# A two-stage kernel on one core: GpSimd's step in the second stage is put in another order

## The chip, the cores and the metric

The kernel runs on one core of a Trainium2 chip. The metric is device time in microseconds (us), the median of the runs shown; everything that the kernel does in one launch counts.

## The reference

`x` is 16 images of 512 channels, 64 x 64 pixels, float32. Two layers follow each other, each with a group normalisation (32 groups of 16 channels) in front and a residual add behind:

```python
x = x + _L0_conv_ref(_gn(x), W, bias)     # 5x5 self-correlation descriptor, 1x1 convolution, relu
x = x + _L1_conv_ref(_gn(x), w1, b1, w2, b2)

def _L1_conv_ref(x, w1, b1, w2, b2):      # KERNELS = 1, 3, 5, 7, 9, 11, 13
    gap = jnp.mean(x, axis=(2, 3))
    hmid = jax.nn.relu(jnp.einsum('bc,ec->be', gap, w1) + b1)
    s = jax.nn.relu(jnp.einsum('be,ce->bc', hmid, w2) + b2)
    q_s = jnp.clip(jnp.floor(s), 0, n_k - 2).astype(jnp.int32)
    q_b = q_s + 1
    ...
    return frac_b * b_out + frac_s * s_out + x   # two max pools of each plane, mixed
```

In the second layer each of the 8192 planes (one channel of one image) gets a score. The score picks two neighbouring pool sizes of the seven, and the result is a weighted sum of the two max-pooled planes and the plane itself.

## The kernel before

**Stage one** (0 to about 2610 us of the span) does the first layer, image by image, and writes each plane twice to device memory: the plane itself (`y_planes`) and the plane after a row-wise maximum (`wide_planes`). **A short middle part** (to about 2690 us) scores the planes, gives each one of six classes (0 to 5, by its smaller pool size), sorts them by class and packs them in tiles of 128 planes of one class. There are 72 tile numbers (`NT`), of which 67 hold planes; the last 5 are empty.

**Stage two** is the one that the change touches. It goes through the tiles, in the order of the classes. Five engines work side by side, each with an instruction order written out by hand, tied by semaphores. Tile `t` uses plane buffer `t % 4` (`bufs`, 4 buffers), and there is one `source` buffer only. What each does:

- GpSimd (`POOL`) issues the transfers, all of them indirect DMAs of its own queue. `gather(t, b)`: clears the record slot (L506), copies the tile's plane numbers (L507), waits for that copy, reads the tile's class, then issues the gather of the records (L511) and of the planes (L514, 128 rows of 16 KB). `gather_source(t, b)`: waits until ScalarE has taken the source of the tile before (`s_ypad`), copies indices (L528), issues the gather of row maxima into `source` (L531). For classes 2 to 5 this is 128 rows of 16 KB, for classes 0 and 1 all rows but one are out of bounds. `scatter(t, b)`: waits for the eight results of the tile (`s_res`), then issues the write to `out` (L539), again 128 rows of 16 KB. In front of `gather(t + 2)` the engine waits until the scatter of tile `t - 2`, which had the same buffer, has landed (`written`).
- ScalarE (`ACT`), in its step `t`: `pad_plane(t + 1)` copies tile `t + 1` into the padded buffer `ypad` (L673 to L675), out of its own plane buffer for classes 0 and 1 and out of `source` for the others. Then `results(t - 1)` moves the eight finished banks of tile `t - 1` from PSUM to its buffer (L695), and `diagonals(t + 1)` makes the weights (L687, L688).
- VectorE (`DVE`) computes the two pools of a tile from `ypad` as a chain of elementwise maxima (all at L1062), 6 to 12 of them by class. It starts when `ypad` is ready. Half-way it has no more need of `ypad` and says so (`s_rows`).
- TensorE (`PE`) mixes: per bank two matmuls (class 0) or three (L1403, L1405, L1407), each one instruction of the program and two records of the trace. Bank `b` of a tile waits until ScalarE has emptied it of the tile before.

`pad_plane` starts with the three waits on which much rests:

```python
act.wait_ge(gathered[u], turns_done(t, u))   # record and plane gathers of tile t landed
if not (isinstance(t, int) and t == 0):
    act.wait_ge(s_rows, t)                   # VectorE has done with ypad of tile t - 1
act.wait_ge(sourced, (t + 1) * 16)           # source gather of tile t landed
```

GpSimd's order of a step is given by the function `step`:

Of the kernel before, what the change touches and what calls it, by code (L numbers as in the profile page):

```python
# [41 lines left out]
BUFS = 4  # L42
# [46 lines left out]
def build(nc, x, wt, wturn, bias, w1t, b1, w2t, b2, consts, out):  # L89
# [5 lines left out]
    NT = -(-(NC + NCLS - 1) // BUFS) * BUFS  # L95
# [15 lines left out]
    with ctx:  # L111
# [328 lines left out]
        def _(pool):  # L440
# [60 lines left out]
            def class_of(t):  # L501
                return pool.value_load(cls_i[0:1, bass.ds(t, 1)], min_val=0, max_val=NCLS)  # L502

            def gather(t, b):
                pool.sem_inc(s_issue, 1)
                pool.memset(recs_in[:, b, :], 0.0)  # L506
                pool.tensor_copy(idx[:, b:b + 1], ids_i[:, bass.ds(t, 1)]).then_inc(s_idx, 1)  # L507
                pool.wait_ge(s_idx, t + 1)
                pool.sem_inc(s_issue, 1)
                with pool.If(class_of(t) < NCLS):  # L510
                    pool.indirect_dma_start(out=recs_in[:, b, :], out_offset=None, in_=rec_dram[:, :],  # L511
                                            in_offset=bass.IndirectOffsetOnAxis(ap=idx[:, b:b + 1], axis=0),
                                            bounds_check=NPL - 1, oob_is_err=False).then_inc(gathered[b], 16)
                    pool.indirect_dma_start(out=bufs[:, b, :], out_offset=None, in_=y_dram[:, :],  # L514
                                            in_offset=bass.IndirectOffsetOnAxis(ap=idx[:, b:b + 1], axis=0),
                                            bounds_check=NPL - 1, oob_is_err=False).then_inc(gathered[b], 16)
                with pool.Else():
                    pool.dma_start(bufs[0:1, b, 0:REC], rec_dram[0:1, :]).then_inc(gathered[b], 16)
                    pool.dma_start(recs_in[0:1, b, :], rec_dram[0:1, :]).then_inc(gathered[b], 16)

            def gather_source(t, b):

                if not (isinstance(t, int) and t == 0):
                    pool.wait_ge(s_ypad, t)
                    pool.sem_inc(s_issue, 1)
                    pool.wait_ge(sourced, t * 16)
                pool.sem_inc(s_issue, 1)
                pool.tensor_copy(src_idx[:, b:b + 1], src_ids[:, bass.ds(t, 1)]).then_inc(s_src, 1)  # L528
                pool.wait_ge(s_src, t + 1)
                pool.sem_inc(s_issue, 1)  # L530
                pool.indirect_dma_start(out=source, out_offset=None, in_=wide_dram[:, :],  # L531
                                        in_offset=bass.IndirectOffsetOnAxis(ap=src_idx[:, b:b + 1], axis=0),
                                        bounds_check=NPL - 1, oob_is_err=False).then_inc(sourced, 16)

            def scatter(t, b):
                pool.wait_ge(s_res, (t + 1) * 8)
                pool.sem_inc(s_issue, 1)  # L537
                with pool.If(class_of(t) < NCLS):  # L538
                    pool.indirect_dma_start(out=out_rows[:, :],  # L539
                                            out_offset=bass.IndirectOffsetOnAxis(ap=idx[:, b:b + 1], axis=0),  # L540
                                            in_=bufs[:, b, :], in_offset=None,
                                            bounds_check=NPL - 1, oob_is_err=False).then_inc(written[b], 16)
                with pool.Else():
                    pool.dma_start(no_out[bass.ds(t, 1), :], bufs[0:1, b, 0:REC]).then_inc(written[b], 16)  # L544

            def step(t, u):

                if not (isinstance(t, int) and t + 1 >= NT):
                    gather_source(t + 1, (u + 1) % BUFS)
                if not (isinstance(t, int) and t < 2):  # L550
                    pool.wait_ge(written[(u + 2) % BUFS], ((t - 2) // BUFS + 1) * 16 if isinstance(t, int)
                                 else turn_of(t, u - 2))
                if not (isinstance(t, int) and t + 2 >= NT):
                    gather(t + 2, (u + 2) % BUFS)
                if not (isinstance(t, int) and t < 1):
                    scatter(t - 1, (u - 1) % BUFS)

            gather(0, 0)
            gather_source(0, 0)
            gather(1, 1)  # L560
            for u in range(BUFS):
                step(u, u)
            with pool.Fori(1, NT // BUFS - 1) as g:
                def turn_of(t, back):

                    return (g + (1 if back >= 0 else 0)) * 16
                for u in range(BUFS):
                    step(g * BUFS + u, u)
            for u in range(BUFS):
                step(NT - BUFS + u, u)  # L570
# [867 lines left out]
```

## Time and profile before

| | |
|---|---|
| median of 3 runs | 4451.67 us (4446.97 to 4456.05) |
| the profiled execution | 4448.36 us |
| its span | 4446.7 us |
| busy in the span: TensorE, VectorE, ScalarE, GpSimd | 88%, 80%, 43%, 51% |
| stage two with its tail, from the first L673 (2687.3 us) to the end of the span | 1759 us |

The span is the profiled part of one execution; the execution's own time is 1.7 us longer. Engines of the trace are PE (TensorE), PEld (its weight loads), DVE (VectorE), ACT (ScalarE), POOL (GpSimd) and SP. L531 is line 531 of the kernel. A row of a timeline has the start, the duration, the engine, line and operation; in brackets stands the engine's idle time before it and what ended it.

### The profile page before, as it was taken

The numbers are of one execution on the slowest core, as the hardware profiler recorded it, in microseconds if no ns is written. First come the engines' busy times: TensorE is split into PE (matmuls) and PEld (weight loads), VectorE is DVE, ScalarE is ACT, GpSimd is POOL, SyncE is SP. The second block draws the span as 40 slices with busy tenths as digits, with TensorE's granted clock in tenths as the row PEclk, the third lists the DMA queues.
The fourth block names the chain that finished last, engine by engine and source line by source line (L and its number), as shares of the span: only waits on it lengthen the run. The fifth ranks groups of instructions, "written<-read, shape, count | busy, mean of one in ns | idle before, by whom it ended". The sixth has DMA issues, their size and how long they took to land. (4 is left out here: it accounts for less than half of the span.)

```text
span 4446.7 us, 76741 instructions
## 1 busy us (share of the span) xinstructions
PE 3932.6 (88%) x23656; PEld 2159.5 (49%) x23657; DVE 3557.4 (80%) x3528; ACT 1897.6 (43%) x2964; POOL 2279.6 (51%) x1793
## 2 busy tenths in 40 slices
PE   5999999999999999999999965789888888888785
PEld 3556555555555555655566642334333333333332
DVE  5878888788887878888888766699866799999993
ACT  3444444444454544444444403443433333433332
POOL 3555555555555655555565514355544444556442
PEclk9999999999999999999999977899998999989897
DMA  4444344544544444444453334545555566565551
GB/s 183 151 173 176 137 168 167 176 150 156 195 149 159 173 150 167 177 150 155 176 173 132 121 79 172 202 174 190 198 219 234 197 234 246 227 243 211 224 212 50
DMA packets 252235, 781.08 MB, mean 176 GB/s; under 512 B 98150, under 2 KB 98150, under 8 KB 229990
## 3 DMA queue, kind: packets, MB, share of 16 engines
q1 hardware_dynamic: 219600, 417.85, 26.9%
q0 software_dynamic: 32288, 358.95, 20.9%
q8 instruction: 176, 2.88, 0.3%
q14 instruction: 171, 1.40, 0.1%
HBM read 428.22 MB, written 409.08 MB: 188 GB/s over the span
## 5 line engine op out<-in xcount | busy, mean ns | idle before, releaser
L1062 DVE TENSOR_TENSOR arena<-arena 128x2048 f32<-128x2048 f32 (+5 forms) x539 | 1442.4, 2695 | 262.2 <-ACT arena L675 223.0
L1403 PE MATMUL psum<-arena 128*128 128x512 f32 x1072 | 608.3, 651 | 293.4 <-ACT arena L695 213.0
L1208 PE MATMUL psum<-arena 128*128 128x256 f16 (+1 forms) x6344 | 754.6, 273 | 57.4 <-DVE arena L808 44.2
L447 POOL TENSOR_TENSOR arena<-arena 128x512 f16<-128x512 f32 x512 | 720.8, 1415 | 147.1 <-ACT arena L597 141.0
L1231 PE MATMUL psum<-arena 128*128 128x512 f16 x2048 | 776.5, 379 | 0.0
L1233 PE MATMUL psum<-arena 128*128 128x512 f16 x2048 | 776.2, 379 | 0.0
L1232 PE MATMUL psum<-arena 128*128 128x512 f16 x2048 | 776.2, 379 | 0.0
L673 ACT ACTIVATE arena<-arena 128x4096 f32 x67 | 242.4, 3619 | 1051.7 <-issue 1051.7
L1208 PEld LDWEIGHTS psum<-arena 128*128 128x128 f16 x6344 | 600.3, 101 | 177.6 <-DVE arena L808 71.7
L456 POOL TENSOR_TENSOR arena<-arena 128x512 f32 (+1 forms) x512 | 635.0, 1272 | 9.0 <-ACT arena L611 6.2
L820 DVE BATCH_NORM_STATS2 bny<-arena 128x6 f32 (+1 forms) x512 | 355.6, 694 | 340.0 <-POOL arena L456 326.7
L611 ACT ACTIVATE arena<-psum,bias_sb 128x512 f32<-128x512 f32 x512 | 338.1, 686 | 581.3 <-POOL arena L456 380.1
L1407 PE MATMUL psum<-arena 128*128 128x512 f32 x1072 | 578.9, 623 | 0.0
L466 POOL CAST arena<-arena 128x128 f16<-128x128 f32 x128 | 37.3, 291 | 999.3 <-DVE arena L852 999.3
L1403 PEld LDWEIGHTS psum<-arena 128*128 128x128 f32 x1072 | 216.1, 208 | 589.7 <-issue 316.7
L1405 PE MATMUL psum<-arena 128*128 128x512 f32 x896 | 494.2, 635 | 0.0
L595 ACT ACTIVATE arena<-arena,gbias,grstd 128x512 f32 (+1 forms) x512 | 413.3, 807 | 48.6 <-POOL arena L447 45.9
L597 ACT ACTIVATE arena<-arena,gbias,grstd 128x512 f16 (+1 forms) x512 | 411.3, 803 | 0.0
L539 POOL DMA_INDIRECT out<-arena x67 | 115.4, 1722 | 544.2 <-issue 544.2
L1407 PEld LDWEIGHTS psum<-arena 128*128 128x128 f32 x1072 | 218.0, 203 | 287.7 <-issue 287.7
L808 DVE TENSOR_TENSOR arena<-psum,cst 128x256 f32<-128x256 f32 x496 | 287.1, 579 | 74.8 <-PE psum L1208 60.3
L695 ACT ACTIVATE arena<-psum,arena 128x512 f32<-128x512 f32 x536 | 319.0, 696 | 57.5 <-PE psum L1407 46.0
(161 smaller groups left out, 4324.0 us busy)
## 6 DMA issues: line engine op xcount, KB each, us to landing
arena<-in_x SPq DMA_DIRECT2D x64, 2048.0 KB, 13.2
wide_planes<-arena SPq DMA_DIRECT2D x128, 1024.0 KB, 5.4
y_planes<-arena SPq DMA_DIRECT2D x64, 2048.0 KB, 7.6
arena<-arena SPq DMA_DIRECT2D x1536, 8.0 KB, 1.8
arena<-wide_planes,arena POOLq DMA_INDIRECT x72
arena<-plane_records,arena POOLq DMA_INDIRECT x67
arena<-y_planes,arena POOLq DMA_INDIRECT x67
out<-arena POOLq DMA_INDIRECT x67, 7.9
```

The lines of the kernel that those rows point to most:

```text
L447: pool.tensor_tensor(gl[:, ct, slot], g32[:, ct % 2, :], gh[:, ct, slot], ALU.subtract).then_inc(s_gl, 1)
L456: pool.tensor_tensor(y, y, relu[:, o % 2, :], ALU.add).then_inc(s_added, 1)
L595: act.activation(g32[:, ct % 2, :], piece, ACT.Identity, bias=gbias[:, ct:ct + 1], scale=grstd[:, ct:ct + 1])
L597: act.activation(gh[:, ct, (c % RING) * CW:(c % RING + 1) * CW], piece, ACT.Identity, bias=gbias[:, ct:ct + 1], scale=grstd[:, ct:ct + 1]) ...
L1062: ins = dve.tensor_tensor(dst, a, b, ALU.max)
L1208: return pe.matmul(dst, w, m, start=(k == 0), stop=(k == nk - 1))
L1231: pe.matmul(dst, h, gh[:, ct, slot], start=(ct == 0), stop=False)
L1232: pe.matmul(dst, h, gl[:, ct, slot], start=False, stop=False)
L1233: last = pe.matmul(dst, l, gh[:, ct, slot], start=False, stop=(ct == CT - 1))
L1403: pe.matmul(dst, diag[:, s, 0, :], bufs[:, u, b * CW:(b + 1) * CW], start=True, stop=False)
L1405: pe.matmul(dst, diag[:, s, 1, :], small[:, s, b * ROWS:(b + 1) * ROWS, 1:W + 1], start=False, stop=False)
L1407: pe.matmul(dst, diag[:, s, 2, :], big[:, s, b * CW:(b + 1) * CW], start=False, stop=True)\
```

## The change

Only GpSimd's program changes, in `step` and in the lines in front of the loop. A step had: source gather of the tile one ahead; wait for the scatter of tile `t - 2`; record and plane gathers of the tile two ahead; scatter of tile `t - 1`. It now has: source gather of the tile two ahead; scatter of tile `t - 1`; wait for the scatter of tile `t - 2`; record and plane gathers of the tile two ahead. The source gather of tile 1 is issued in front of the loop. The number of transfers and their sizes stay as they were, and no wait is added to or taken from the helpers.

```diff
             def step(t, u):
 
-                if not (isinstance(t, int) and t + 1 >= NT):
-                    gather_source(t + 1, (u + 1) % BUFS)
+                if not (isinstance(t, int) and t + 2 >= NT):
+                    gather_source(t + 2, (u + 2) % BUFS)
+                if not (isinstance(t, int) and t < 1):
+                    scatter(t - 1, (u - 1) % BUFS)
                 if not (isinstance(t, int) and t < 2):
                     pool.wait_ge(written[(u + 2) % BUFS], ((t - 2) // BUFS + 1) * 16 if isinstance(t, int)
                                  else turn_of(t, u - 2))
                 if not (isinstance(t, int) and t + 2 >= NT):
                     gather(t + 2, (u + 2) % BUFS)
-                if not (isinstance(t, int) and t < 1):
-                    scatter(t - 1, (u - 1) % BUFS)
 
             gather(0, 0)
             gather_source(0, 0)
             gather(1, 1)
+            gather_source(1, 1)
```

## Rows read from the trace of the kernel before

**Rows 1.** Busy time by stretch (window, length, engines, PEclk, DMA, GB/s): classes 0 to 5.

```profile
2735.20:2925.70 190.50, 147.45 (x293) 61.91 (x291) 127.12 (x56) 89.41 (x136) 73.81 (x63) 0.87 0.51 199
2925.70:3189.10 263.40, 238.18 (x516) 103.16 (x517) 248.67 (x88) 109.77 (x165) 149.06 (x80) 0.93 0.50 185
3189.10:3523.40 334.30, 278.43 (x589) 119.16 (x587) 215.93 (x72) 119.19 (x180) 162.25 (x85) 0.91 0.55 213
3523.40:3806.80 283.40, 243.15 (x528) 104.35 (x528) 258.89 (x99) 109.30 (x166) 123.54 (x77) 0.95 0.62 237
3806.80:4094.70 287.90, 248.01 (x519) 106.26 (x520) 273.01 (x88) 109.22 (x166) 172.46 (x77) 0.91 0.58 225
4094.70:4337.80 243.10, 198.10 (x419) 84.81 (x418) 239.29 (x106) 90.08 (x136) 105.22 (x65) 0.91 0.57 218
```

**Rows 2.** Waits of 2735 to 4338 us; last row: who waited for L531, whole span.

```profile
ACT arena L673 <- issue: 972.0, 64, 18.9
...
POOL arena L506 <- DMA out<-arena: 140.2, 49, 6.8
...
  ACT arena L673: 1043.9, 66
```

**Rows 3.** Timeline of ScalarE over one tile of class 2.

```profile
3329.64 3.62 ACT L673 ACTIVATE arena<-arena 128x4096 f32 x1 [17.89 <-issue]
...
3333.47 0.40 ACT L675 ACTIVATE arena<-arena 128x256 f32 x1
3333.77 4.72 ACT L695 ACTIVATE arena<-psum,arena 128x512 f32<-128x512 f32 x8
...
3357.20 3.62 ACT L673 ACTIVATE arena<-arena 128x4096 f32 x1 [17.60 <-issue]
```

**Rows 4.** Timeline of GpSimd over the same tile.

```profile
3340.14 1.87 POOL L539 DMA_INDIRECT out<-arena  x1 [9.23 <-issue]
3342.02 1.34 POOL L528 COPY arena<-arena 128x1 int32 x1
3344.29 4.53 POOL L531 DMA_INDIRECT arena<-wide_planes,arena  x1 [0.93 <-POOL arena L528]
3348.82 0.12 POOL L506 MEMSET arena<- 128x4 f32 x1
3348.87 3.52 POOL L507 COPY arena<-arena 128x1 int32 x1
3353.99 1.04 POOL L511 DMA_INDIRECT arena<-plane_records,arena  x1 [1.59 <-issue]
3355.33 0.99 POOL L514 DMA_INDIRECT arena<-y_planes,arena  x1 [0.30 <-issue]
```

**Rows 5.** VectorE in that tile: timeline, then its forms (busy, mean ns), in 3334 to 3352.5 us.

```profile
3334.11 18.24 DVE L1062 TENSOR_TENSOR arena<-arena 128x2112 f32<-128x2112 f32 x6 [9.62 <-ACT arena L675]
...
L1062 DVE TENSOR_TENSOR arena<-arena 128x4096 f32<-128x4096 f32 x2 | 8.8, 4424 | 0.2
L1062 DVE TENSOR_TENSOR arena<-arena 128x2048 f32<-128x2048 f32 x3 | 6.8, 2290 | 0.1
L1062 DVE TENSOR_TENSOR arena<-arena 128x2112 f32<-128x2112 f32 x1 | 2.4, 2359 | 9.6 <-ACT arena L675 9.6
```

**Rows 6.** Further VectorE forms: one tile of class 3, then one of class 4.

```profile
L1062 DVE TENSOR_TENSOR arena<-arena 128x1024 f32<-128x1024 f32 x3 | 3.6, 1223 | 0.1
L1062 DVE TENSOR_TENSOR arena<-arena 128x2176 f32<-128x2176 f32 x1 | 2.4, 2426 | 0.0
...
L1062 DVE TENSOR_TENSOR arena<-arena 128x2240 f32<-128x2240 f32 x1 | 2.5, 2491 | 0.0
```

**Rows 7.** L514 (ns: min/median/max) in the stretch of class 2, then of class 3.

```profile
L514 POOL DMA_INDIRECT arena<-y_planes,arena x13: 993/993/993, 3189.1 to 3521.5; - x13
...
L514 POOL DMA_INDIRECT arena<-y_planes,arena x11: 4104/4109/4112, 3548.6 to 3806.2; - x11
```

**Rows 8.** DMA rate, 3329 to 3358 us, in 40 slices of 0.725 us.

```profile
GB/s 0 2 1 271 113 316 407 497 407 407 429 45 0 0 0 0 0 0 362 362 362 362 362 678 407 0 0 0 271 136 452 429 452 429 384 339 2 1 249 113
```

## The prediction

> **What bounds the kernel now.** Stage one is untouched, so I first read the stretches of stage two [rows 1]. A tile is 15 ScalarE instructions (three of padding, eight of results, four of diagonals), so the stretches hold 9, 11, 12, 11, 11 and 9 tiles of classes 0 to 5, and a tile takes 21.2, 23.9, 27.9, 25.8, 26.2 and 27.0 us. VectorE is full in classes 1 and 5 (94 and 98%), but only 67% busy in class 0 and 65% in class 2, and no other engine is full there. So I read the waits [rows 2]: `pad_plane` (L673) waits 972 us in all, and in 66 of 67 cases what released it was L531, the source gather.
>
> The three timelines of one class 2 tile show the ring that follows. I count from the start of L673 at 3329.64. Padding ends at 4.2 and the results at 8.9 [rows 3]. The scatter starts at 10.5 and ends at 12.4, the index copy L528 at 13.7, the source gather's issue runs from 14.7 to 19.2 [rows 4], and the next L673 starts at 27.6, 8.4 after it (8.7 in the neighbouring tiles; I use 8.7 for the way from the end of an issue of 2 MB to the padding that waits for it). This ring is padding, results, scatter, source gather, padding. The plane gather of the tile behind it is issued at 25.7 to 26.7 and is not needed before the padding one period later: 27 us of slack.
>
> **How VectorE holds GpSimd.** With VectorE idle L514 takes 0.99 us in every case of class 2; in class 3, where a VectorE operation of 4.42 us runs over it, 4.11 [rows 7]. The single cases show the rule. VectorE's operations of the class 2 tile end at 6.8, 9.1, 11.5, 13.7, 18.25 and 22.7 (one of 2.36, three of 2.29, two of 4.42 from 4.47 on, with small gaps) [rows 5]. The copy L528 ends at 13.73 and the copy L507 at 22.75, each 0.05 after an operation's end; the scatter ends at 12.37 and L531 at 19.18, each 0.9 after one; the memset L506 isn't held (0.12) [rows 4]. So a copy lasts until the running operation ends, and an indirect issue until 0.9 after that. The shared port of the page "SBUF — State Buffer" of the Trainium skill is the name for this, but its section "Who interferes with whom" infers that a `tensor_tensor` does not hold descriptor generation. By it the indirect issues would take about 1 us always; the rows of L514 and L531 speak against it. It is rival B below.
>
> **The change, part by part.** Removed: GpSimd's wait for a landed scatter in front of L506, 140 us over 49 cases [rows 2]. It is beside the ring (the plane gather behind it has its slack), so it is worth nothing. In the new order the scatter of tile t - 2 is a whole period old when it is asked for, so this wait is gone.
>
> Moved forward: the source gather of tile t + 2 now waits only for the padding of t + 1. The end of padding comes at 4.2; L528 has some queue instructions in front of it, VectorE starts at 4.47, so I let the copy lose that race and be held to the end of the first operation. Bound: it wins, and the issue is over one operation sooner.
>
> Moved back: record and plane gathers of t + 2 now stand behind the scatter of t - 1, and that waits for results which ScalarE starts only after padding t + 1. Padding t + 2 waits for these gathers too. So there is a new ring: padding, results, scatter, L507, L511, L514, landing, padding. What was covered by 27 us of slack is now on it. In the rows its fixed parts are: 10.5 to the scatter's start, 1.6 from L507's end to L511, 0.3 from there to L514 [rows 4], 8.7 to the padding; between them each issue is held by the rule above. By class, ends counted from L673:
>
> Classes 0 and 1 (first operations 2.29 each, ends 6.8, 9.1, 11.3, 13.8, 16.1, 18.4): L528 to 6.8, L531 7.7 to 10.0, scatter 10.5 to 12.2, L507 to 13.9, L511 15.5 to 17.1, L514 17.4 to 19.3, next padding at 28.0. Nine tiles: 252.0 - 190.5 = +61.5. Eleven: 308.0 - 263.4 = +44.6.
>
> Class 2: L528 to 6.9, L531 to 10.0, scatter to 12.4, L507 to 13.7, L511 15.3 to 19.2, L514 19.5 to 23.6, padding at 32.3. Twelve tiles: 387.6 - 334.3 = +53.3.
>
> Class 3 starts with an operation of 4.42, then 2.43, three of 1.22, two of 2.29 [rows 5, 6]: ends 8.9, 11.4, 12.6, 13.9, 15.0, 17.3, 19.5. L528 to 8.9, L531 9.9 to 12.3, scatter to 13.5, L507 to 13.9, L511 15.5 to 18.3, L514 18.6 to 20.5: 29.2. Here the DMA queue decides. The slices show bursts of some 6.5 us for a gather (9 slices) and 5.1 for a scatter (7 slices) [rows 8]. Source, scatter and plane gather now follow each other in one queue within 9 us; if they run one behind the other, the padding comes at 12.3 + 8.7 + 5.1 + 6.2 = 32.3, and a burst that needs no start-up of its own saves about 1 us, so 30.3 to 32.3. I take 31.5. Eleven tiles: 346.5 - 283.4 = +63.1.
>
> Class 4 (4.42, 2.49, 2.42, three of 2.29 [rows 5, 6]: 8.9, 11.4, 13.9, 16.2, 18.5, 20.7): L531 to 12.4, scatter to 14.8, L507 to 16.3, L511 17.9 to 19.4, L514 19.7 to 21.6: 30.3; by the queue 30.4 to 32.4. I take 31.5 again: 346.5 - 287.9 = +58.6.
>
> Class 5: L531 to 10.0, plane issue to about 19.8: 28.5; by the queue 28.0 to 30.0; I take 29.2. VectorE needs 27 to 28 for such a tile, so it no longer bounds it, and the lead that padding had before the stretch's end, some 8.7 us, need not be worked off in the tail: 9 x 29.2 - 243.1 - 8.7 = +11.
>
> In front of class 0 the first two rings come from 13 and 22 us to about 22 and 30: +17, an estimate from the same parts. The five empty tiles at the end move nothing of size: 0.
>
> Sum: 61.5 + 44.6 + 53.3 + 63.1 + 58.6 + 11 + 17 = +309. The profiled execution takes 4448.4, so 4757; the median of the runs is 3.3 above it: 4760.
>
> The other price in this sum is the transfer. The page "DMA: Bandwidth & Descriptors" of the Trainium skill, section "Anatomy of one DMA — SWDGE (gpsimd) path", fits 2.0 us plus bytes over 436 GB/s; for 2 MB that would be 6.8 us, an estimate, in place of the 8.7 of the rows. With it each ring would be 1.9 us shorter and the sum about 120 us smaller, 4640.
>
> **Bounds.** Low: L528 wins its race in every tile, which ends L531 of classes 3 and 4 at 9.8, and bursts pack well: 28.3 in both, so 22 x 3.2 = 70 less: 4690. High: the scatter's queue instructions (1.66 us from the results to L539) start only when L531 has ended: each issue after it slips by one VectorE operation, 1.3 us in classes 0 to 2, some 2 to 3 in 3 and 4, 1.6 in 5: 32 x 1.3 + 22 x 2.5 + 9 x 1.6 = +111: 4870.
>
> **The rivals.**
> A, the forecast: the plane gather becomes the last thing that padding waits for, 4690 to 4870. Chance 0.88.
>
> B, VectorE does not hold the indirect issues, only the copies. Classes 0 and 1: L507 to 13.9, L514 to 17.8, padding at 26.5; class 2 about 28 by the queue, 3 and 4 about 30, 5 about 28. The sum is 48 + 28 + 0 + 47 + 42 + 0 + 17 = 182: 4634. Speaks against it: L514 and L531 at 4.1 and 4.5 us. Chance 0.05.
>
> C, the other side: the plane gather still lands before the source would have, and only the gain is left. For that its issue has to end by 21.2 - 8.7 = 12.5 in class 0 and by 19.2 in class 2. Then classes 0 to 5 would be bound by mixing and pools, about 17, 23, 23, 24, 25 and 27 us: a gain of 36 + 10 + 58 + 20 + 13 = 137, 4315. Against it: the scatter alone ends at 12.2, with two issues, a held copy and 1.6 us of queue still to come. Chance 0.03, with 0.01 more for no change (the change's two effects cancel).
>
> D, TensorE's clock. It was granted 0.91 of full in class 2 and a tile's 48 records cost 278.4 / 12 = 23.2 us busy [rows 1]. In a period of 32 it fits with room. If the longer idle times let the clock sit at its lower level throughout, a tile costs about 23.2 x 0.91 / 0.5 = 42 us, mixing bounds classes 1 to 5, and 54 tiles at some 46 give well over 5200. Nothing in the rows has it sit there while PE works most of the time. Chance 0.03.
>
> **How the numbers follow.** The likeliest case is A at 4760. The range is 4650 to 4870: the bounds of A, and toward B at the lower end. A change under 0.2% (about 9 us) is not to be told from none. Faster 0.03 (C), same 0.01, slower 0.96 (A, B, D).
>
> **What would show it.** In the changed profile L673 should be released by L514 or its landing and no more by L531; L531 should start some 8 after L673; L506 should wait for no landing; a tile of class 0 should take 28, of class 2 about 32, of 3 and 4 about 31. VectorE's idle time should rise by nearly the sum. I am wrong if the plane gather's issue ends before 17 in class 0, if the 8.7 us don't hold for a plane gather that runs right behind a scatter, or if the scatter starts later than 10.5 where L531 has ended before.

## The result and the profile after

The changed kernel takes 4817.25 us (median of 4 runs), the kernel before 4452.97 us beside it: a ratio of 1.082, 95% interval 1.080 to 1.084. That is 364 us slower; 4760 was forecast, with a range of 4650 to 4870. The profiled execution after has a span of 4811.8 us, 365.1 more than before.

First the stretches of stage two again, by class, as in [rows 1] (window, length, busy time of PE, PEld, DVE, ACT, POOL, then PEclk, DMA share, GB/s):

```profile
2752.10:3012.30 260.20, 146.11 (x288) 61.69 (x288) 131.25 (x56) 89.33 (x135) 103.24 (x63) 0.77 0.37 145
3012.30:3336.70 324.40, 250.78 (x528) 107.44 (x528) 242.61 (x86) 109.21 (x166) 134.28 (x77) 0.88 0.39 150
3336.70:3726.10 389.40, 275.77 (x576) 118.07 (x576) 215.91 (x72) 119.05 (x180) 182.16 (x84) 0.85 0.50 183
3726.10:4080.60 354.50, 252.79 (x528) 108.15 (x528) 261.55 (x99) 109.22 (x166) 138.27 (x77) 0.85 0.50 190
4080.60:4446.10 365.50, 254.03 (x528) 108.72 (x528) 274.94 (x88) 109.13 (x165) 165.81 (x77) 0.84 0.47 177
4446.10:4715.00 268.90, 208.60 (x432) 89.06 (x432) 245.11 (x108) 89.33 (x135) 101.02 (x63) 0.86 0.52 197
```

Every stretch is longer, and no engine's work accounts for it: VectorE is busy 1371.4 us over the six, against 1362.9 before [rows 1], and over the whole span VectorE is busy 3557 us as before, TensorE 28 us more (at a lower granted clock) and GpSimd 41 us more. The time is idle time. Its cause is in the waits of the two gathers (who waited for the line: us, times). L514 first, then L531, whole span:

```profile
  ACT arena L674: 1372.8, 65
...
  ACT arena L674: 71.8, 2
```

L674 is the first instruction of the padding (L673 before; lines behind the diff are one further down). Before, 66 paddings were released by the source gather [rows 2]. Now 65 are released by the plane gather L514 and two by the source gather. The ring of one class 2 tile, which answers to [rows 3] and [rows 4], ScalarE and then GpSimd:

```profile
3369.06 3.62 ACT L674 ACTIVATE arena<-arena 128x4096 f32 x1 [22.44 <-issue]
...
3373.19 4.71 ACT L696 ACTIVATE arena<-psum,arena 128x512 f32<-128x512 f32 x8
...
3401.61 3.62 ACT L674 ACTIVATE arena<-arena 128x4096 f32 x1 [22.59 <-issue]
```

```profile
3373.73 2.20 POOL L528 COPY arena<-arena 128x1 int32 x1 [13.49 <-ACT arena L676]
3376.82 2.29 POOL L531 DMA_INDIRECT arena<-wide_planes,arena  x1 [0.89 <-POOL arena L528]
3379.56 1.86 POOL L539 DMA_INDIRECT out<-arena  x1 [0.46 <-issue]
3381.42 0.12 POOL L506 MEMSET arena<- 128x4 f32 x1
3381.46 1.32 POOL L507 COPY arena<-arena 128x1 int32 x1
3384.52 3.73 POOL L511 DMA_INDIRECT arena<-plane_records,arena  x1 [1.73 <-issue]
3388.55 4.08 POOL L514 DMA_INDIRECT arena<-y_planes,arena  x1 [0.31 <-issue]
```

Counted from 3369.06: L528 ends at 6.9, L531 at 10.0, the scatter at 12.4, L507 at 13.7, L511 at 19.2, L514 at 23.6, the next padding starts at 32.55. GpSimd used to wait 140 us in front of L506 for a landed scatter [rows 2]; there is no such wait in this step. It now waits in front of L528 for the padding, 13.5 us in this tile: nothing is left for it to do meanwhile.

### The profile page after: what moved, and what is told of

It reads as the page before. It is cut to its first block and busy times, and to the rows that moved or that the text cites. A ratio compares the mean times of both kernels' runs of the same rounds, so it can differ in the third digit from the quotient of the medians.

```text
span 4811.8 us, 76741 instructions
## 1 busy us (share of the span) xinstructions
PE 3960.7 (82%) x23656; PEld 2169.7 (45%) x23657; DVE 3557.1 (74%) x3528; ACT 1894.0 (39%) x2964; POOL 2320.5 (48%) x1793
## 3 DMA queue, kind: packets, MB, share of 16 engines
q0 software_dynamic: 32288, 358.95, 19.7%
## 5 line engine op out<-in xcount | busy, mean ns | idle before, releaser
L1404 PE MATMUL psum<-arena 128*128 128x512 f32 x1072 | 624.9, 667 | 633.7 <-ACT arena L696 593.5
L674 ACT ACTIVATE arena<-arena 128x4096 f32 x67 | 242.3, 3616 | 1444.6 <-issue 1444.6
L528 POOL COPY arena<-arena 128x1 int32 (+1 forms) x72 | 191.3, 2657 | 957.0 <-ACT arena L676 942.7
L1408 PE MATMUL psum<-arena 128*128 128x512 f32 x1072 | 581.2, 625 | 0.0
L1406 PE MATMUL psum<-arena 128*128 128x512 f32 x896 | 503.5, 646 | 0.0
```

Of the source, the lines that this page charges most:

```text
L1404: pe.matmul(dst, diag[:, s, 0, :], bufs[:, u, b * CW:(b + 1) * CW], start=True, stop=False)
L1406: pe.matmul(dst, diag[:, s, 1, :], small[:, s, b * ROWS:(b + 1) * ROWS, 1:W + 1], start=False, stop=False)
L1408: pe.matmul(dst, diag[:, s, 2, :], big[:, s, b * CW:(b + 1) * CW], start=False, stop=True)\
```

## The experiments

All are edits of GpSimd's program in stage two, and one of VectorE's. The table gives, for each profile, us per tile of classes 0 to 5, worked out from the starts of the padding's first instruction (the 4th, 13th, 24th, 36th, 47th, 58th and 67th, difference over the number of tiles), and the whole. "-" in place of the interval: one execution. The kernel before, timed beside them, lay between 4438 and 4456 us, so a difference of less than some 15 us says nothing for a single execution. The groups are cut by count and are one tile off at the first two borders: the last tile of group 0 has the pools of class 1, and the last of group 1 those of class 2. Of the edits below, those with words in place of code are outlines.

| run | 0 | 1 | 2 | 3 | 4 | 5 | whole, us | ratio to before |
|---|---|---|---|---|---|---|---|---|
| kernel before | 21.2 | 23.9 | 27.9 | 25.8 | 26.2 | 27.0 | 4453 | 1 |
| changed kernel | 28.9 | 29.5 | 32.5 | 32.2 | 33.2 | 29.9 | 4817 | 1.080 to 1.084 |
| plane_moves_nothing | 22.4 | 23.7 | 26.0 | 27.7 | 27.7 | 27.1 | 4468 | - |
| scatter_moves_nothing | 27.9 | 28.1 | 32.4 | 29.2 | 30.6 | 28.8 | 4714 | - |
| short_pools | 28.4 | 28.6 | 30.0 | 32.1 | 32.4 | 29.8 | 4751 | - |
| prepare_ahead | 28.8 | 28.9 | 32.4 | 32.1 | 31.5 | 28.0 | 4768 | - |
| plane_late_only | 28.7 | 32.6 | 37.2 | 33.5 | 34.7 | 34.5 | 4975 | - |
| plane_before_scatter | 27.8 | 27.5 | 29.5 | 29.0 | 30.0 | 27.7 | 4655 | 1.044 to 1.048 |
| e1_scatter_moves_nothing | 25.8 | 25.7 | 28.3 | 27.0 | 28.0 | 27.5 | 4557 | - |
| plane_source_scatter | 19.7 | 24.3 | 25.8 | 27.5 | 28.6 | 27.6 | 4451 | 0.999 to 1.001 |
| issues_only_old_order | 21.3 | 24.1 | 25.5 | 25.8 | 25.5 | 27.2 | 4412 | 0.990 to 0.993 |
| issues_only | 17.7 | 23.1 | 23.3 | 25.3 | 25.1 | 26.7 | 4331 | 0.972 to 0.975 |

**Does padding wait for the plane's bytes?** plane_moves_nothing edits the gather at L514:

```diff
-                                            bounds_check=NPL - 1, oob_is_err=False).then_inc(gathered[b], 16)
+                                            bounds_check=0, oob_is_err=False).then_inc(gathered[b], 16)
```

> The changed kernel; the plane gather's bounds check lets only plane 0 through, so it is issued as before and moves nothing (the tiles hold stale planes). Theory (padding waits for this gather, 8.7 us after its issue): the wait shrinks to some 4 us as for the small source gathers of the kernel before. Classes 0 and 1 go from 28 to 29.5 us (32.3) to about 23.4 (27.6), class 2 from 32.3 to 27.6, classes 3 and 4 from 32 and 33 to about 26, class 5 to VectorE's 27.8: about 4525 us in all. Rival (the slow tiles come from GpSimd's long issue chain as such, not from a wait for the plane's bytes): the next step starts when it did, 4817.

Measured 4468, 349 below the changed kernel. Classes 0 to 2 lost 5.8 to 6.5 us a tile, more than the 4.7 expected: the padding comes 2.4 to 3.2 us after the end of L514 in all but one tile, not 4. Classes 3 and 4 lost 4.6 and 5.6, less than the 6 or more expected; that fits a scatter which is still queued in front of the gather (in class 3 L514 ends at 20.4, and the padding comes at 27.6). All 63 paddings of the loop are still released by L514 (980.1 us). GpSimd's issue chain goes on as before, so the chain alone does not make the slow tiles: in class 0 it takes some 19 of the 22.4 us that are left, and what brings a tile to 28.9 is the wait for the bytes that it asks for last.

**Is it the scatter's transfer or its place?** scatter_moves_nothing has the same edit at L539.

> The changed kernel; the scatter's bounds check lets only plane 0 through, so it is issued as before and moves nothing (the output is left unwritten). Theory (ring with VectorE's hold): the scatter costs its place in GpSimd's order and not its transfer, except where the plane gather is queued behind it. Classes 0, 1, 2 unchanged (28 to 32 us), class 3 from 32.2 to 29.1, class 4 from 33.2 to about 31.5, class 5 from 29.9 to 28.6: about 4755 us. Rival (queue): each tile loses the scatter's 5 us, some 315 in all, about 4500 us.

Measured 4714. Class 2 unchanged (32.4), class 3 down by 3.1 to 29.2, class 4 by 2.7 (33.24 to 30.58), class 5 by 1.1: the theory, not the queue alone, by which each tile would have lost 5 us. But class 1 fell too, from 29.5 to 28.1, and class 0 by 1.0, where the theory expected no change. The reason is in GpSimd's reading of the tile's class (L502), here over class 1 (ns, min/median/max), of the changed kernel and then of this run:

```profile
L502 POOLq TENSOR_LOAD <-arena x22: 292/306/899, 3021.4 to 3318.5; - x22
```

```profile
L502 POOLq TENSOR_LOAD <-arena x22: 291/294/305, 3011.7 to 3293.2; - x22
```

With the scatter's bytes on their way the read behind it takes up to 0.9 us in place of 0.3. That brings L511's start from 15.4 to between 15.9 and 16.3 us behind the padding, on top of the start of VectorE's next operation. Two tiles of class 1 of the changed kernel, with padding at 3068.09 and at 3160.69:

```profile
3084.09 3.18 POOL L511 DMA_INDIRECT arena<-plane_records,arena  x1 [2.23 <-issue]
3087.58 4.09 POOL L514 DMA_INDIRECT arena<-y_planes,arena  x1 [0.31 <-issue]
...
3176.69 1.06 POOL L511 DMA_INDIRECT arena<-plane_records,arena  x1 [2.22 <-issue]
3178.06 1.82 POOL L514 DMA_INDIRECT arena<-y_planes,arena  x1 [0.30 <-issue]
```

L511 starts 16.00 us behind the padding's start in both. In the first L511 just misses and is held to the end of the operation, and L514 then runs into one of 4.42 us: 32.3 us for the tile. In the second it gets through: 28.0 us. A few hundredths of a microsecond decide over 4 us.

**VectorE's hold.** short_pools cuts the last two operations of a tile to one row:

```diff
-                    op(inner, sm_[:, :, 0:W], sm_[:, :, 2:W + 2])
-                    op(bg, hbuf[:, PADR - 1:PADR - 1 + H, :], hbuf[:, PADR + 1:PADR + 1 + H, :], signal=s_pool)
+                    op(inner[:, 0:1], sm_[:, 0:1, 0:W], sm_[:, 0:1, 2:W + 2])
+                    op(bg[:, 0:1], hbuf[:, PADR - 1:PADR, :], hbuf[:, PADR + 1:PADR + 2, :], signal=s_pool)
```

> The changed kernel; the last two maxima of a tile of classes 1 to 5 work on one row of the 64 (the pools come out wrong), so VectorE's two operations of 4.42 us at the end of a tile are gone and no longer hold GpSimd. Theory: in class 1 the tiles of 32.3 us vanish (all 28 to 29.5), in class 2 the plane gather is issued by 17.7 instead of 23.6 and the queue decides at about 30, class 3 stays at 32.2, class 4 loses its tiles of 35 us: about 4765 us. Rival (the hold plays no part, only the order): 4817.

Measured 4751. L514 in class 2, which took 4.08 us above:

```profile
L514 POOL DMA_INDIRECT arena<-y_planes,arena x12: 984/990/997, 3339.5 to 3669.3; - x12
```

Class 2 went to 30.0, where the queue decides (in the tile at 3380.65 the scatter lands at 23.5, the plane gather 4.8 later and 10.2 after the end of its issue), and the tiles of 32.3 in class 1 and of 35 in class 4 are gone, as expected. VectorE's `tensor_tensor` does hold an indirect issue; its work as such was never the bound here.

**The copy taken away from behind the scatter.** prepare_ahead moves L506 and L507 in front of it:

```diff
                     gather_source(t + 2, (u + 2) % BUFS)
+                    wait for written[t - 2]; memset and index copy of t + 2
                     scatter(t - 1, (u - 1) % BUFS)
                     gather(t + 2, (u + 2) % BUFS)
```

> The changed kernel; the clearing of the record slot and the index copy (L506, L507) of tile t+2 are moved in front of the scatter of t-1, so that behind the scatter only the two issues stand. Theory (ring with the hold): L511 starts right behind the scatter, the plane gather's issue ends near 17 in classes 0 and 1, so they take about 26 us and lose their tiles of 29.5 and 32.3; in classes 2 to 5 the queue behind source and scatter decides, 30, 32.2, 32.4 and 29.9. Sum about 100 us less than the changed kernel, 4713. Rival (the copy and the reading of the class are hidden anyway): 4817.

Measured 4768, half of the expected gain, and the mechanism was wrong in classes 0 to 2. GpSimd in a tile of class 0 with padding at 2837.65 (L541 is the scatter, L513 and L516 the record and plane gathers):

```profile
2847.68 1.30 POOL L507 COPY arena<-arena 128x1 int32 x1
2849.16 3.12 POOL L541 DMA_INDIRECT out<-arena  x1 [0.17 <-POOL arena L507]
2852.58 2.04 POOL L513 DMA_INDIRECT arena<-plane_records,arena  x1 [0.31 <-issue]
2854.93 1.85 POOL L516 DMA_INDIRECT arena<-y_planes,arena  x1 [0.31 <-issue]
```

The copy was held to 11.3, so the scatter started 0.2 us after the end of a VectorE operation in place of 0.8 before one, and was held for the whole of the next one. What the copy gave up behind the scatter it took in front. L516 ends at 19.1, as in the changed kernel, and not at 17. The 49 us come mostly from classes 4 and 5 (some 20 and 17 us), where 9 and nothing were expected, and 7 from class 1, where the three tiles of 32.3 are gone.

**Each half of the change alone.** plane_late_only is the kernel before with the plane gather behind the scatter:

```diff
                     gather_source(t + 1, (u + 1) % BUFS)
+                    scatter(t - 1, (u - 1) % BUFS)
                     wait for written[t - 2]
                     gather(t + 2, (u + 2) % BUFS)
-                    scatter(t - 1, (u - 1) % BUFS)
```

> The kernel before with one half of the change: record and plane gathers of t+2 stand behind the scatter of t-1, the source gather keeps its old place (source t+1 after the padding of t, which is behind the plane gather of the step before). Theory (the plane gather behind the scatter binds, the early source gather pays something where it has 2 MB to bring): classes 0 and 1 stay at the changed kernel's 28.9 and 29.5 us, since their source gather is tiny and lands in 4 us; in classes 2 to 5 the source gather comes last, queued behind the plane gather, at about 38, 38, 39 and 33 us. About 5045 us in all, 230 above the changed kernel. Rival (the loss comes from the source gather moved early, which fills the queue in front of the scatter): with the source gather back in its place this is faster than the changed kernel, 4600 or less.

Measured 4975: the late plane gather alone costs 522 us, and the early source gather wins back 158 of them, not the 230 expected. All 63 paddings of the loop are released by the source gather (1498.0 us). Class 1 was expected at 29.5 and came to 32.6: L528 and the tiny source gather stand behind L514 in VectorE's two operations of 4.42 us (in the tile at 3097.52 L531 ends 28.1 us behind the padding's start), which I had left out. In classes 3 and 4 the paddings came some 4.4 us earlier than I had added up. In the trace, with no source gather in front of it, the scatter starts at 10.5 and not at 12.6, L514 ends at 18.2 in class 3 and not at 20.4, and the source gather, issued until 24.9, lands 7.1 us later, with the scatter and the plane gather already landed (at 18.3 and 25.2; tile at 3908.18).

plane_before_scatter keeps the early source gather and puts the plane gather next:

```diff
                     gather_source(t + 2, (u + 2) % BUFS)
-                    scatter(t - 1, (u - 1) % BUFS)
                     wait for written[t - 2]
                     gather(t + 2, (u + 2) % BUFS)
+                    scatter(t - 1, (u - 1) % BUFS)
```

> The changed kernel with GpSimd's step in the order source gather t+2, record and plane gathers t+2, scatter t-1: only the scatter is moved behind the plane gather. Theory (ring): padding of t+2 waits for the plane gather of t+2, and the scatter in front of it is part of that ring. The issue of the plane gather should end near 16.9 us after L674 in classes 0 and 1 (19.2 now), 19.2 in class 2, 18.2 in class 3, 19.4 in class 4, so tiles take about 25.6, 25.6, 27.9, 27, 28 and 27.8 us and the whole about 4560 us. Rival (queue): the slowdown comes from three transfers that follow each other closely in one DMA queue, whatever their order; then nothing changes, 4817.

Measured 4655, so the scatter's place in the ring costs 162 us and not 260. L514 ended where expected (16.9 in class 0), but the padding came 10.8 us later and not 8.7. e1_scatter_moves_nothing is this order with the scatter moving nothing:

> The order source, plane, scatter of the run plane_before_scatter, whose tiles of class 0 took 27.7 us where 25.6 was expected (10.8 us from the end of the plane gather's issue to the padding in place of 8.7); here the scatter moves nothing. Theory A: the scatter issued right behind the plane gather shares the DMA engines with it and delays its landing; then class 0 comes to 25.7, class 2 from 29.0 to 27.9, class 3 to about 27.2, and the whole to about 4540 us. Theory B: the delay is of the issue itself (two issues on GpSimd close together); then class 0 stays at 27.7 and the whole near 4640.

Measured 4557, and class 0 came to 25.8: theory A. L514 takes 1.97 us in both runs, so the issue isn't delayed. The plane gather is still on the ring, and a scatter issued right behind it delays its landing by 1.8 to 2.1 us in classes 0, 1, 3 and 4, in class 2 by 1.2. That the two share the DMA engines fits, but only the delay is shown.

**The plane gather gets its lead back.** plane_source_scatter:

```diff
-                    gather_source(t + 2, (u + 2) % BUFS)
-                    scatter(t - 1, (u - 1) % BUFS)
                     wait for written[t - 2]
                     gather(t + 2, (u + 2) % BUFS)
+                    gather_source(t + 2, (u + 2) % BUFS)
+                    scatter(t - 1, (u - 1) % BUFS)
```

> The changed kernel with the step in the order wait for the scatter of t-2, record and plane gathers t+2, source gather t+2, scatter t-1. The source gather keeps its early place and the plane gather gets its lead back, so the cycle is source, scatter, plane gather of one tile later. Theory (ring): no transfer has to wait for results and then be waited for in the same period; tiles become bound by mixing, pools and the queue, about 18, 23, 23, 24.5, 25.5 and 27.8 us, the whole about 4340 us, 2.5% below the kernel before. Rival (queue): source, scatter and plane gather still run one behind another within one period, so it is not faster than the kernel before, 4450 or more.

Measured 4451, the same as the kernel before (ratio 0.999 to 1.001), and not the 4340 expected. The source gather is early and the plane gather has its slack, but a third ring takes over. A class 2 tile, padding at 3354.21:

```profile
3357.57 0.10 POOL L506 MEMSET arena<- 128x4 f32 x1 [13.25 <-DMA out<-arena]
3357.70 0.18 POOL L507 COPY arena<-arena 128x1 int32 x1
3359.50 2.48 POOL L511 DMA_INDIRECT arena<-plane_records,arena  x1 [1.61 <-issue]
3362.29 1.94 POOL L514 DMA_INDIRECT arena<-y_planes,arena  x1 [0.31 <-issue]
3364.24 1.50 POOL L528 COPY arena<-arena 128x1 int32 x1
3366.63 2.16 POOL L531 DMA_INDIRECT arena<-wide_planes,arena  x1 [0.89 <-POOL arena L528]
3369.10 4.26 POOL L539 DMA_INDIRECT out<-arena  x1 [0.30 <-issue]
3384.04 0.10 POOL L506 MEMSET arena<- 128x4 f32 x1 [10.68 <-DMA out<-arena]
```

GpSimd waits 10 to 13 us for the scatter that it has just issued, since the next plane gather goes into the buffer that this scatter empties. Then come four issues and two copies, all but the first copy held by VectorE for some time, and L531 ends at 14.6 where it could end at 10.0. The ring is landing, plane gather, source gather, scatter, landing: 26.5 us.

**The third ring shortened.** issues_only keeps that order and takes everything out of the ring that is no issue. Gather and scatter get index columns of their own, so that no copy has to wait for the landed scatter:

```diff
             def step(t, u):
+                prepare(t + 2, ...)          # index copies of both gathers of t + 2
+                prepare_scatter(t, ...)      # index copy of the scatter of t
+                # class of t + 2 is read here, and only then the wait for written[t - 2]
                 gather(t + 2, ...)           # memset, L511, L514
                 gather_source(t + 2, ...)    # issue alone
                 scatter(t - 1, ...)
```

> The order plane, source, scatter of the run plane_source_scatter (4451 us, ring: the scatter of t-2 has landed, plane gather, source gather, scatter, landing; 26.6 us in class 2), with all index copies and the reading of the class of t+2 in front of the wait for the landed scatter, so that behind it stand only the clearing of the record slot and the three issues. Theory (that ring binds): it gets about 4.6 us shorter and falls below what pools and mixing need: about 18, 23, 23, 24.5, 25.5 and 27.8 us for classes 0 to 5, 4340 us in all, 2.5% below the kernel before. Rival (the DMA queue binds, three transfers of 2 MB in a row and landings that delay each other): classes 2 to 4 stay at 26 to 29 us and the whole is 4440 or more.

Measured 4331 (ratio 0.972 to 0.975), 122 us below the kernel before and the fastest version here. The source gather's issue now ends at 12.3 in class 2. VectorE is busy 1359.5 of the 1487.4 us of the six stretches, 91%.

How much of this is the order? issues_only_old_order has the same helpers in the order of the kernel before.

> The kernel before, in its own order (source t+1, plane t+2, scatter t-1), with the index copies and the reading of the class in front of the wait for the landed scatter as in the run issues_only. It tells what of the 120 us that issues_only gains is the order. Theory (the old ring padding, results, scatter, source gather, padding is only shortened by one copy and one hold): L531 follows the scatter at once and ends near 14.7 us after the start of the padding; class 0 about 18.6 us, class 1 23.2, class 2 about 26 (the source is queued behind the scatter), class 3 25.3, class 4 25.8, class 5 27: about 4390 us. Rival (the copies are all of it): as issues_only, 4331.

Measured 4412 (0.990 to 0.993), expected 4390. So the helpers alone give 0.9% and the order, on top of them, another 80 us; without them the order gave nothing (plane_source_scatter, 4451). Class 0 was expected at 18.6 and stayed at 21.3, class 1 at 24.1; the gain is in class 2 (25.5, 28 us in all) and class 4 (8 us). In class 0 the source gather's issue did end 2.4 us earlier (14.6 behind the padding's start, 17.1 before), but it is in the queue right behind the scatter, and in each tile of class 0 it lands 0.2 to 1.5 us after the scatter, 4.7 to 6.0 after the end of its issue. The same one-row gather, with no scatter still moving in front of it, lands 1.8 to 2.2 us after that end in the changed kernel. So it waits for the scatter; an edit that tries this alone wasn't run.

## Why the prediction was right

**What changes hands.** The step on which all rests, that the plane gather takes the source gather's place as the last thing padding waits for, is shown by the waits (65 to 2) and by plane_moves_nothing. Rival C (the gather in time all the same) and D (TensorE's clock) fell: PEclk was 0.84 to 0.88 in classes 1 to 5 and 0.77 in class 0, between its levels of 1.2 and 2.4 GHz on average, and no longer period was set by the mixing: padding was always released by a gather. Rival B (VectorE holds no issue) fell with L511 and L514 at 3.7 and 4.1 us and with short_pools. The inference of the page "SBUF — State Buffer" of the Trainium skill, section "Who interferes with whom", weighed in the prediction, does not hold for these indirect issues: L514 takes 4.08 us under an operation of 4.42 and 0.99 where short_pools takes that away.

**The chain of a tile.** Class 2, forecast and measured: L528 6.9 and 6.9, L531 10.0 and 10.0, scatter 12.4 and 12.4, L507 13.7 and 13.7, L511 19.2 and 19.2, L514 23.6 and 23.6, padding 32.3 and 32.5. The copy L528 lost its race with VectorE by 0.2 us, as assumed (3373.73 against 3373.53). In class 3 the fit is as close: L531 12.3, scatter 13.6, L514 20.4. The "27 us of slack" of the plane gather were its lead: from the end of its issue at 26.7 [rows 4] to the padding that needed it, two periods of 27.7 on, were some 29 us, and 8.7 of them are the transfer's own way, so the slack was some 20. No term of the sum uses it.

**The terms of the sum**, forecast and measured from the spans:

| | forecast | measured |
|---|---|---|
| in front of class 0 | +17 | +16.9 |
| class 0 | +61.5 | +69.8 |
| class 1 | +44.6 | +60.9 |
| class 2 | +53.3 | +55.2 |
| class 3 | +63.1 | +71.1 |
| class 4 | +58.6 | +77.7 |
| class 5 and tail | +11 | +13.7 |
| sum | +309 | +365.3 |

**What was mis-sized.** The mechanism held; the sum was 56 us short, every stretch by a little.
- The step from L507's end to L511, "1.6" in the forecast. It was 2.2 in classes 0, 1 and 4, since the read of the class is slow behind a moving scatter, and in 4 of 9, 3 of 11 and 4 of 11 tiles L511 then misses its gap: L514 starts at 19.5 in place of 17.4 in classes 0 and 1, and at 22.0 in place of 19.8 in class 4. These tiles make some 32 of the 56 us. scatter_moves_nothing, where the read is fast, gives 27.9 and 28.1 for classes 0 and 1, the 28.0 of the forecast. One more tile of class 4, at 4281.11, took 34.8 us: there L511 is in time and L514 is late (21.4), and it is just as slow in scatter_moves_nothing, so its cause is another and stays open.
- The border of class 1: the last three tiles of its group took 25.1, 30.5 and 32.1 us and not 28.0. In the first the plane gather lands 4.3 us after its issue and not 7.1, in the second the source gather issued for the next class already moves 2 MB, and the third has the pools of class 2. Together some 4 us.
- Class 3: "a burst that needs no start-up of its own saves about 1 us, so 30.3 to 32.3. I take 31.5". The tile takes 32.2, the upper end: 8 us in all, and 6 more in those tiles of class 4 that missed nothing (32.4). The DMA rate in a tile of class 3 (3886 to 3919 us, 40 slices of 0.825 us) shows one unbroken stretch:

```profile
GB/s 0 0 0 0 0 0 0 0 0 0 0 0 0 0 0 0 318 278 377 496 377 199 179 278 358 417 477 417 457 417 400 457 417 417 457 397 40 0 0 0
```

The landings tell more. From the start of the issue to the landing, in class 3, L531, then L539, then L514:

```profile
DMA to landing us min/median/max: 10.5/10.9/11.4
DMA to landing us min/median/max: 12.4/13.2/13.6
DMA to landing us min/median/max: 11.5/12.1/12.5
```

With the starts at 9.8, 12.6 and 18.6 the source gather lands at 20.8, the scatter at 25.7 and the plane gather at 30.6, and 1.6 us later the padding starts. So the plane gather did save its start-up: 4.9 us behind the scatter, where the forecast's largest value had 6.2. But the source gather landed 8.5 us after the end of its issue and not 7.1 (7.2 where the scatter moves nothing): the scatter queued behind it delays it, as in plane_before_scatter. That 32.2 met the 32.3 of the working is two errors of over 1 us that cancel, which is luck. That the queue sets this term is shown by scatter_moves_nothing (29.2).
- Class 5: 29.9 for 29.2, the same choice inside the queue's range of 28.0 to 30.0: 6 us more, of which the tail gave 3 back.

The price of 8.7 us from the end of an issue to the padding held for a plane gather behind a scatter that had landed (8.8 in the class 1 tile at 3160.69). It has two parts: 7.1 us to the landing and 1.6 from the landing to the padding's start. By the page "DMA: Bandwidth & Descriptors" of the Trainium skill, section "Anatomy of one DMA — SWDGE (gpsimd) path", the transfer takes 6.8 us, an estimate; the trace agrees with it to 0.3 us from the end of the issue (from its start it is 8.8 in class 0). The prediction set that figure against a way that runs on to the padding, so the 120 us between its two sums are mostly that second part.

## What to carry to other kernels

Before an operation is moved ahead on an in-order queue, ask of each one that it overtakes who waits for it and how much slack it has: here some 20 us of slack were spent, and more, to start another transfer 7 us sooner. A buffer that is refilled as soon as its last user has landed ties store and load into a ring of their own; whatever is no issue (index copies, a look at a flag) belongs in front of the wait. And where one engine's instructions are held to the ends of another's, the cost of a step is not its own duration but the next gap that it catches, so a tenth of a microsecond can be worth four, and a copy moved away can come back as a missed gap.

## What the runs showed of the hardware that was not expected

- GpSimd's load of one value of SBUF into a register took 0.3 us while no scatter moved, and up to 0.90 us in classes 0 and 1 while one did (1.22 at most, in class 2). In the changed kernel 53 of stage two's 140 loads took more than 0.4 us, with the scatter moving nothing none. A gather of 2 MB doesn't do it: in class 4 of scatter_moves_nothing the load takes 0.29 us at 16.5, and the source gather lands at 19.5. That these loads share a path with the scatter is only argued.
- An indirect issue of GpSimd is held at its start only: one that starts within the operation that is running ends 0.9 us after that operation, and VectorE's next operation, already started, does not hold it again (class 2: L531 runs from 7.8 to 10.0, VectorE's operations end at 9.1 and 11.4).
- A scatter issued 0.3 us after the plane gather delays that gather's landing by 2.0 us (10.8 against 8.8 us from the end of its issue, plane_before_scatter and e1_scatter_moves_nothing), though the gather was first in the same queue. Where three transfers of 2 MB follow each other closely (class 3 of the changed kernel), the first lands 8.5 us after the end of its issue and each of the others 4.9 us after the one before.
